# Two expert layers computed for the two chosen experts of each token only: rows scattered by expert, 39 tiles of 128 slots, rows gathered back

## What is computed

```python
# third layer's expert part: hidden width F2 = 512
g = softmax(LN(t) @ gate_w + gate_b)          # [2048, 8]
g = where(g among its row's top 2, g, 0)
y = sum_e g[:, e] * (gelu(LN(t) @ w1[e] + b1[e]) @ w2[e] + b2[e])
# fourth layer's: hidden width F3 = 256, the two gates are normalised to sum 1
y = sum_e g[:, e] * ((silu(LN(t) @ w1[e]) * (LN(t) @ w3[e])) @ w2[e])
t = t + y
```

## Time and profile before

| | |
|---|---|
| time of 3 runs | 659.5 us median, 658.87 to 660.37 |
| the profiled execution | span 660.2 us; of it nothing else is timed |
| granted clock, mean | 0.842 |
| PE / DVE / ACT / POOL busy | 92% / 81% / 61% / 22% of the span |
| DMA queues | 28.78 MB moved, 12.3% of the 16 engines' time |

### The profile page before, as it was taken

The page is one execution under the profiler, slowest core; times in us unless marked ns, Lnnn a source line. Parts: engine busy times, 40 slices in busy tenths (PEclk is TensorE's granted clock), DMA queues, the critical chain, the costliest instruction groups (busy, mean ns, idle before and its releaser), DMA issues. The chain is left out here.

```text
span 660.2 us, 10008 instructions
## 1 busy us (share of the span) xinstructions
PE 610.4 (92%) x3182; PEld 483.8 (73%) x3182; DVE 533.9 (81%) x1153; ACT 400.6 (61%) x793; POOL 146.2 (22%) x117
## 2 busy tenths in 40 slices
PE   9999977998899999999997899999967989999996
PEld 4786555886678888887886777777746678888784
DVE  2537479976788778878788799999997799999987
ACT  4523121103778888888873799999974455555553
POOL 1092455763421101111011211111103011111200
PEclk9597586998899999999998555555557899999999
DMA  5000000002132210221000000000001152122201
GB/s 183 1 0 1 0 1 0 1 1 65 42 122 95 97 67 30 95 95 54 11 1 0 1 2 0 0 0 0 1 2 49 51 180 87 75 84 90 81 33 42
DMA packets 9987, 28.78 MB, mean 44 GB/s; under 512 B 992, under 2 KB 3296, under 8 KB 9824
## 3 DMA queue, kind: packets, MB, share of 16 engines
q1 hardware_dynamic: 9952, 28.34, 12.3%
HBM read 27.15 MB, written 1.18 MB: 43 GB/s over the span
## 5 line engine op out<-in xcount | busy, mean ns | idle before, releaser
L1343 DVE TENSOR_TENSOR hL<-hraw,hH 128x1024 fp32r<-128x1024 f32 (+1 forms) x128 | 131.4, 1053 | 34.4 <-ACT hH L1069 33.8
L1154 PE MATMUL ps<-xH,wH 128*128 128x512 f32 x256 | 103.4, 404 | 5.4 <-DVE xL L1219 2.5
L1073 ACT ACTIVATE hraw<-ps,bias 128x512 f32<-128x512 f32 x128 | 86.7, 686 | 28.8 <-PE ps L1156 27.0
L1155 PE MATMUL ps<-xL,wH 128*128 128x512 f32 x256 | 102.6, 401 | 0.0
L1156 PE MATMUL ps<-xH,wL 128*128 128x512 f32 x256 | 102.5, 400 | 0.0
L1001 POOL TENSOR_TENSOR wL<-wraw,wH 128x1024 fp32r<-128x1024 f32 (+1 forms) x16 | 35.7, 2229 | 230.4 <-DVE wH L1207 230.4
L1166 PE MATMUL ps<-hH,wH 128*128 128x512 f32 x192 | 76.0, 396 | 6.0 <-DVE hL L1343 6.0
L1168 PE MATMUL ps<-hH,wL 128*128 128x512 f32 x192 | 75.4, 393 | 0.0
L1167 PE MATMUL ps<-hL,wH 128*128 128x512 f32 x192 | 75.3, 392 | 0.0
L1069 ACT ACTIVATE hH<-hraw 128x1024 fp32r<-128x1024 f32 x64 | 67.5, 1055 | 1.0
L1078 ACT ACTIVATE hraw<-ps 128x512 f32<-128x512 f32 x64 | 38.3, 600 | 48.9 <-PE ps L1156 47.4
(11 more groups left out here) (248 smaller groups left out, 1200.7 us busy)
## 6 DMA issues: line engine op xcount, KB each, us to landing
G<-gates_scratch SPq DMA_DIRECT2D x30, 512.0 KB, 4.7
wraw<-in_ex SPq DMA_DIRECT2D x8, 514.5 KB, 6.3
wraw<-in_ex SPq DMA_DIRECT2D x8, 384.0 KB, 5.1
w<-in_pack SPq DMA_DIRECT2D x1, 1420.5 KB, 8.5
xs<-in_x SPq DMA_DIRECT2D x4, 256.0 KB, 4.8
G<-gates_scratch SPq DMA_DIRECT2D x4, 256.0 KB, 3.5
out<-acc SPq DMA_DIRECT2D x4, 256.0 KB, 2.1
w<-in_pack SPq DMA_DIRECT2D x1, 501.0 KB, 3.7
```

What stands on the lines that cost most here:

```text
L1073: act.activation(hraw[:, k % 2, h, :], ps[:, h, :], ACT.Gelu, bias=bias[:, place(k, last)[0], h:h + 1]).then_inc(z["act"], 1)
L1154: pe.matmul(o, wH[:, p, at:at + P], xa, start=True, stop=False)
L1155: pe.matmul(o, wH[:, p, at:at + P], xb, start=False, stop=False)
L1343: dve.tensor_tensor(hL[:, k % 2, g * half:(g + 1) * half, :], src, hi.bitcast(F32), ALU.subtract).then_inc(z["hl"], 1)
```

## The change

The expert layers compute only chosen pairs of token and expert.

- DRAM gets `slots_in` (8 regions of 2048 rows, one an expert, and one of spare tiles) and `slots_out` (39 x 128 rows). SP zeroes `slots_in` once, at the start.
- After the gates, a token's place in its expert's region is the count of tokens of that expert ahead of it: a matmul with a triangle of ones for its own group of 128 rows and one with a matrix of ones for each earlier group, in two halves of the tokens. POOL then scatters the rows of `xc` by 32 indirect DMAs of 128 rows of 512 bytes.
- DVE makes two tables for NT = 39 tiles of 128 slots: which expert a tile has, and where it lies. 39 tiles hold any split of 4096 pairs over 8 experts ((4096 + 8 x 127) / 128); all 39 are always computed.
- For each tile SP reads the tile's place into a register and loads 128 rows, PE transposes them, ACT and DVE make high and low, PE makes the up product with the tokens as the stationary operand and the expert's weights moving, by an address from a register that PE reads from the table; activation; PE transposes the hidden rows (4 or 2 transposes); high and low again; PE makes the down product; DVE adds its two halves; SP stores the tile.
- The rows of a token's two slots are gathered by 32 indirect DMAs of POOL and added to `t` with their gates by DVE (`combine`). In layer 3 this is done in the next block; in layer 4 it is followed by transposes, copies and the DMAs out.
- All 8 experts' weights of a layer stay in SBUF and are split beforehand: layer 3's in `block2` (ACT high, POOL low), layer 4's while layer 3's tiles run (DVE high, POOL low).

```diff
-                for j, k, last in rounds(pe):
-                    if not (last and k == 2 * NCH - 1):
-                        up(j, k + 1, last)
...
-                    down(j, k, last)
...
+        def gather(pool, layer, c):
+            for b in (2 * c, 2 * c + 1):
+                for s in range(S):
+                    for k in range(TOPK):
+                        pool.indirect_dma_start(y_rows(k, s, b), None, ys_d[:],
+                                                bass.IndirectOffsetOnAxis(idy[:, row(layer, s, b), k:k + 1], 0)).then_inc(gathered[c], 16)
...
+                for g in range(2):
+                    pool.wait_ge(z["idx"], z0["idx"] + g + 1)
...
+                    for r in range(GR * g, GR * (g + 1)):
+                        s, b = place(layer, r)
+                        for k in range(TOPK):
+                            pool.indirect_dma_start(xs_d[0:E * T], bass.IndirectOffsetOnAxis(idx[:, r, k:k + 1], 0),
+                                                    xc[:, s, b, :], None).then_inc(z["sc"], 16)
...
+                def load(j):
+                    if j >= NXG:
+                        sp.wait_ge(z["xt"], z0["xt"] + j - NXG + 1)
+                    sp.dma_start(xg[:, j % NXG, :], slot_rows(xs_d, tile_row(j))).then_inc(ld[j % NXG], 16)
...
+                sp.wait_ge(z["tab"], z0["tab"] + 1)
+                sp.wait_ge(z["sc"], z0["sc"] + 16 * TOPK * R)
...
+                def up(j):
+                    e = tile_expert(j)
+                    pe.wait_ge(z["xl"], z0["xl"] + j + 1)
+                    if j >= 2:
+                        pe.wait_ge(z["act"] if layer == 0 else z["hm"], j - 1)
+                    o = ps[:, HB + j % 2, :]
+                    wh, wl = (wHL[:, bass.ds(e, 1), i, 0:up_cols].rearrange("p a n -> p (a n)") for i in range(2))
+                    if layer == 0:
+                        pe.matmul(o, oh[:, j:j + 1].to_broadcast([2 * E, P]), biases[:, 0:up_cols], start=True, stop=False)
+                    pe.matmul(o, xa[:, j % NX, :], wh, start=layer == 1, stop=False)
+                    pe.matmul(o, xb[:, j % NX, :], wh, start=False, stop=False)
+                    pe.matmul(o, xa[:, j % NX, :], wl, start=False, stop=True).then_inc(z["up"], 1)
...
+                def hidden_transposed(j):
...
+                    for h in range(hc):
+                        x = pe.transpose(ps[:, HTB + j % 2, h * P:(h + 1) * P], hraw[:, j % 2, h * P:(h + 1) * P], ident)
...
+                def down(j):
+                    e = tile_expert(j)
...
+                    for h in range(hc):
...
+                        pe.matmul(o.rearrange("p (i n) -> p i n", i=2), hH[:, j % 2, h * P:(h + 1) * P], both, start=h == 0, stop=False)
...
+                        x = pe.matmul(o[:, 0:P], hL[:, j % 2, h * P:(h + 1) * P], wHL[:, bass.ds(e, 1), 0, cols].rearrange("p a n -> p (a n)"),
...
+                for p in range(NT + 2):
+                    if p < NT:
+                        up(p)
+                    if 1 <= p < NT + 1:
+                        hidden_transposed(p - 1)
+                    if p >= 2:
+                        down(p - 2)
+                    if p + 2 < NT:
+                        transposed(p + 2)
...
+                centred(0)
+                masked(0)
+                centred(1)
+                slots(0)
+                masked(1)
+                slots(1)
+                tables()
+                gates()
...
         @block4.gpsimd
         def _(pool):
+            gather(pool, 0, 0)
+            gather(pool, 0, 1)
+            pair_pool(pool, 0)
+            gather(pool, 0, 2)
+            pair_pool(pool, 1)
+            gather(pool, 0, 3)
             pair_pool(pool, 2)
             pair_pool(pool, 3)
...
+            summed(0)
+            summed(1)
+            pair_apply(dve, 0)
+            pair_low(dve, 0)
             for n in range(4):
                 lower(*fragment(0, 0, n), bank=n)
...
+            pair_apply(dve, 1)
+            summed(2)
+            pair_low(dve, 1)
+            summed(3)
             pair_apply(dve, 2)
             centre(0, 0)
```

More of the change, by code:

```diff
@@ new lines, in combine, with row @@
+        def combine(dve, layer, c):
+            dve.wait_ge(gathered[c], (layer + 1) * 16 * 2 * S * TOPK)
+            for k in range(TOPK):
+                for b in (2 * c, 2 * c + 1):
+                    for s in range(S):
+                        x = dve.scalar_tensor_tensor(t[:, s, b, :], y_rows(k, s, b), gk[:, row(layer, s, b), k:k + 1],
+                                                     t[:, s, b, :], ALU.mult, ALU.add)
+                chv.done(x)
+                chv.wait()
+        def row(layer, s, b):
+            return s * B + b if layer == 0 else b * S + s
@@ L914, in experts @@
+        gathered = [sem(f"ex_gathered{c}") for c in range(NCH)]
+        def experts(layer, wHL, n_up, hid, gate_w, gate_b):
             hc = hid // P
-            wcols = (n_up + 1) * hid
-            n_bias = hc + 1 if layer == 0 else 0
+            up_cols = n_up * hid
             room.close()
-            R = S * B
+            R, GR = S * B, S * B // 2
             lg = own(f"lg_{layer}", [P, R, E])
             pg = own(f"pg_{layer}", [P, R, E])
+            rk = own(f"rk_{layer}", [P, R, E])
+            sel = own(f"sel_{layer}", [P, R, TOPK, E])
@@ L931, in experts @@
[L931 to L945, removed]
@@ L946, in experts @@
-            zw = [[sem(f"ex{layer}_{n}{p}") for n in ("w", "ga", "gb")] for p in range(2)]
-            fin = {n: sem(f"fin{layer}_" + n) for n in ("tp done" if layer == 0 else "st").split()}
+            maskb = own(f"maskb_{layer}", [P, R + 1, E], BF16)
+            counts = own(f"counts_{layer}", [P, E])
+            many = own(f"many_{layer}", [P, E, TROWS // E])
+            ntile, ctile, spare = own(f"ntile_{layer}", [P, E]), own(f"ctile_{layer}", [P, E]), own(f"spare_{layer}", [P, E])
+            upto = own(f"upto_{layer}", [P, E, E])
@@ L1093, in _ @@
+                if layer == 1:
+                    for c in range(NCH):
+                        act.wait_ge(z["ftp"], z0["ftp"] + c + 1)
+                        act.activation(outT[:, c, :], ps[:, c, :], ACT.Copy).then_inc(z["fo"], 1)
             @blk.tensor
             def _(pe):
-                LGB = 6
                 def logits(r, columns):
-                    return pe.matmul(ps[:, LGB, r * E:(r + 1) * E], columns, wc(gate_w), start=True, stop=True)
+                    return pe.matmul(ps[:, LGB[r // GR], r * E:(r + 1) * E], columns, wc(gate_w), start=True, stop=True)
@@ new lines, in _ @@
+                if layer == 1:
+                    for c in range(NCH):
+                        combine(dve, layer, c)
+                        dve.sem_inc(z["fin"], 1)
+        room.close()
+        wHL3 = ctx.enter_context(nc.sbuf_tensor("wHL3", [P, E, 2, 3 * F3], F32R, side="right"))
+        wraw3 = nc.alloc_sbuf_tensor_at("wraw3", [P, E, 2, 3 * F3], F32, offset=nc.sbuf_top)
+        experts(0, wHL2, 1, F2, "gate2", "gateb2")
+        room.close()
+        first_weights.close()
+        xH, xL = own("xH", [P, T], F32R), own("xL", [P, T], F32R)
```

674 lines of the change are left out of this document (324 added, 350 removed).

## The result

| | kernel before | changed kernel |
|---|---|---|
| times | 657.6 to 660.4, median 659.2 us | 745.5, 751.1, 795.8, 839.2 us, median 773.5 |
| profiled execution | span 660.2 | span 837.2 (the 839.2 us run) |
| granted clock, mean | 0.842 | 0.623 |

The changed kernel is slower: its two lowest times stand to those of before as 1.135 (95% interval 1.130 to 1.140).

A forecast was written before the change was run, and what follows sets the result against it. The expert stages were taken to be bound by PE time. Layer 4's experts starting at 415.9 + 64c, plus 111.6 + 64c, gave 527.5 + 128c; with c = 1.1, less 0.7, that is 668 us, range 616 to 740.

The forecast's parts named there:

- c: Time one indirect DMA of 128 rows holds POOL; taken as 1.1 us, with the kernels equal at 1.04.
- First scatter: Layer 3's routing, from the norm's end at 160.3 to POOL's first scatter: at 167.7 us.
- First up product: Layer 3: 32 scatters, then 6.2 us to the first tile's up product on PE, at 173.9 + 32c.
- the chain of 6.2: After layer 3's scatters: landing, SP's read and issue, second landing, transpose, high and low parts: 6.2 us.
- Layer 3's tiles: 39 tiles paced by PE at 2.25 us, 88 us, plus start, last chain and store; stage ends at 270.4 + 32c.
- Rival 3: Clock stays at half in both layers' tiles: +53 and +13 us, 735 us; 11%, shared with both rivals or c above 1.3.
- Rival 2: PE's two register reads a tile aren't covered, 0.5 us each: +39 and +18 us, 725 us; chance 14%.
- Gathers to `centre(0, 0)`: Start of the block after layer 3: 32 gathers, landing, additions, moments and `pair_apply`; `centre(0, 0)` at 279.5 + 64c.
- Attention: Fourth layer's attention: 137.2 us as before, less 0.8 for transposes and copies of tokens at its end.
- Layer 4: Its expert stage: routing, scatters, 39 tiles at 1.9 us, gathers and output: 111.6 + 64c.
- Edits at nothing: Zeroing `slots_in` (26 to about 50 us) hidden; POOL's low parts in `block2` cost 0, at most 2 us.

The follow-up runs named there:

- deep bias matmuls: Changed kernel with layer 3's two bias matmuls per tile run over all 128 rows instead of 16, the rest filled with zeros: 720.5 us.
- the first one with `keep_busy`: Changed kernel with unread 512-column matmuls issued on PE after every second scatter in both layers: 837.3 us.
- the one with fixed addresses: Changed kernel with each tile's weights taken from expert j mod 8 instead of an expert number read into a register: 808.8 us.

## Why the prediction was wrong

Slower was right (chance 0.53); the time was outside its range, 616 to 740, in every execution. On the scale of the profiled span it said 668.3; the trace has 837.2, 169 us more. That slower came true is in part the forecast's own reason: with the c that was measured its sum gives 688. But most of the distance has another cause. Step by step, on that trace, where a term holds 32c or 64c with the measured c, since c's own miss is counted once:

- *First scatter*, 167.7: 174.95, 7.2 later. The routing itself was right. The block before ended late (162.7 instead of 156.0 us), because POOL's low parts weren't free: I had looked whether they fit in POOL's idle time and not at what runs beside them on DVE.
- *c*, 1.1: 1.27 and 1.25. 128 times the difference is 20 us. It was within its bounds; the row taken (SP's issue doubled) was a guess in a wide gap, and the share of 0.30 between two issues has no row before.
- *First up product*, 173.9 + 32c: with the two above 221.7; measured 222.3. The landings, SP's issue and the chain of 6.2 were right within 0.6.
- *Layer 3's tiles*: 96.5 us from the first product to the first gather; measured 222.3 to 446.2, 223.9: 127 us too little. This is the step that failed: the tiles were priced at full clock, and ran at 0.50 throughout. At full clock (the run with deep bias matmuls) the same stretch takes 106.5 us (223.1 to 329.6), so that 10 us are the pace and 117 the clock. The pace: 2.59 us a tile instead of 2.25, in part since the pairs of 256 and 128 columns take 0.23, not 0.20 (291.39 to 291.62), and the reads 0.12. (The prediction's own terms add up to 2.27.)
- *Rival 3* named it, with 11% together with others, and had it wrong twice. Its price was counted by columns (3.6 us a tile), although my own 2.25 at full clock weren't columns alone: twice that is 4.5, and measured was 5.69. And its argument against, that the products use the whole array, looked past the two matmuls that the diff shows with 16 rows (`[2 * E, P]`), and that I had priced by their columns alone, at 0.23 and 0.09. The Trainium skill's rule on transposes (TensorE: Matmul & The Clock Gate, "Part 4: PE-mode transpose"), by which these would pull to half clock, isn't what decides here: with deep bias matmuls the five transposes of each tile are still there, at 0.99.
- *Rival 2*: a read holds PE's queue for about 0.6 us, near the 0.5 taken, but it isn't covered in layer 4: its tiles take 2.31 us, where the rival said 2.36, and 1.49 without reads and register addresses, 26 us of the layer. In layer 3 it is covered, but for 0.12. The rival was right for one layer, and the forecast's own pace there (1.9, from a chain on DVE) erred the other way: without reads the median is below it. So the miss is 2.31 - 1.9 = 0.41 us a tile, 16 us. The Trainium skill's floor for a `tensor_load` ("DMA: Bandwidth & Descriptors", "Latency and other measured facts") is about 600 ns; the rows show 0.30 for the load alone, and about 0.6 for the whole read with its register work. My inference from it, that two reads are just covered, fails: they stand in the queue where PE has nothing left to run.
- *Gathers to `centre(0, 0)`*, 9.1 + 32c = 49: 446.2 to 494.4, 48.2. *Attention*, 136.4: 138.5. *Layer 4*, 111.6 + 64c = 192: 204 (633 to 837), of it 16 from the tile.
- *Edits at nothing*: the zeroing of 8.9 MB took 30 us to land, within the estimate of 26 to 50, and was hidden.

7 + 20 + 127 - 1 + 2 + 12 = 167 of the 169 us. Without the 117 us of the clock the same sum gives 718 (668 + 7 + 20 + 10 - 1 + 2 + 12), and the profile of the kernel with deep bias matmuls spans 721.2 (its median is 720.5): even then 9% slower, since less work for PE had been bought with time in which PE waits.

What stays open: why some executions of kernels with the 16-row matmuls get their clock back early (744 to 751 us) and others don't; no profile fell on one of these, and the only trace in which it came back has it at the very end of the stage. Two of the kernels with them, the first one with `keep_busy` and the one with fixed addresses, were long in all four executions. Only 16 and 128 rows were tried, and always among matmuls of 128 rows, so neither is shown at what depth the clock holds, nor whether it is the depth itself or the change from one depth to the other. And whether the fourth layer's attention stays at 0.50 in all kernels for the same reason (its scores are 32 rows deep) wasn't tried.

## What to carry to other kernels

Look at how many rows each matmul uses before you count on the full clock, and try to pad a short contraction with zeros: here 112 rows of zeros cost no time that shows (720.5 us, against 719.3 without these matmuls at all) and gave back at least 25 us. A serial issue on one engine (indirect DMAs at 1.27 us each, register reads at about 0.6 where nothing is left in the queue ahead of them) that stands between two dense stretches is paid in full or nearly; count it as path, not as beside other work. And work put on POOL can be paid by DVE when both run: check what DVE does in the same microseconds.

## What the runs showed of the hardware

- A stage in which PE is never idle can stay at half clock for 221 us: two matmuls of 16 rows among the 18 of a tile were enough. In layer 4, among 12 a tile, they made 4.41 us a tile where the same columns at 128 rows took 2.35. A full clock at the first tile was gone within its first microsecond.
- With such matmuls most kernels weren't only slow but unsteady: 744 to 840 us; padded, 719.8 to 723.1. Two others were steady at the long end (837.1 to 837.5 and 807.6 to 809.5).
- A DVE operation of 0.34 us beside a POOL subtraction took up to 2.39 us, and POOL's issue of an indirect DMA grew from 0.97 to 1.07 us beside DVE's subtractions.
- A register read holds PE's queue for about 0.6 us, and one fewer took 0.59 us off a tile of 2.31; the trace names less than half of what two cost, with the register addresses, as idle for issue (0.36 of 0.82 us).
